# Attention with scratch-turned probabilities: a latent-attention and MoE layer on one NeuronCore

## What is computed

```python
q = heads(xn @ wq.T)                  # 16 heads of 64
latent = xn @ w_kv_down.T             # 64 wide, shared by all heads
k, v = heads(latent @ w_k_up.T), heads(latent @ w_v_up.T)
q, k = rotary(q), rotary(k)
scores = q @ k.T / 8 + causal_mask
probs = softmax(scores)               # float32
attention = concat(probs @ v) @ wo.T
# experts: sigmoid routing, top 4 of 16 (2 of 4 groups), up, silu, down,
# plus a shared expert of 256
```

## Time and profile before

| | us |
|---|---|
| span of the profiled execution (first to last instruction) | 640.2 |
| median of three runs | 641.15 |
| PE busy | 615.5 (96%) |
| DVE busy | 434.6 (68%) |
| ACT busy | 429.5 (67%) |
| POOL busy | 361.1 (56%) |

### The profile page before, as it was taken

The page is one execution under the profiler, slowest core; times in us unless marked ns, Lnnn a source line. Parts: engine busy times, 40 slices in busy tenths (PEclk is TensorE's granted clock), DMA queues, the critical chain, the costliest instruction groups (busy, mean ns, idle before and its releaser), DMA issues.

```text
span 640.2 us, 17380 instructions
## 1 busy us (share of the span) xinstructions
PE 615.5 (96%) x5302; PEld 511.2 (80%) x5302; DVE 434.6 (68%) x1250; ACT 429.5 (67%) x1036; POOL 361.1 (56%) x456
## 2 busy tenths in 40 slices
PE   2899999899999999999999999999999999999996
PEld 2666767688888888888888888888888888888884
DVE  5495556487758775877577757775777677766661
ACT  3364323377776777677767776877687768776763
POOL 2013111168846884688468846884688468843431
PEclk9599999999999999999999999999999999999999
DMA  9500004942484248324832483248424832483001
GB/s 256 147 21 2 1 1 106 205 108 47 106 207 97 46 105 210 90 49 103 210 89 49 104 211 86 50 106 210 118 53 103 211 84 54 102 212 84 2 2 34
DMA packets 35208, 65.29 MB, mean 102 GB/s; under 512 B 11104, under 2 KB 19312, under 8 KB 35056
## 3 DMA queue, kind: packets, MB, share of 16 engines
q1 hardware_dynamic: 32624, 63.53, 41.4%
q10 hardware_dynamic: 2560, 1.45, 0.9%
HBM read 5.84 MB, written 1.05 MB: 11 GB/s over the span
## 4 chain that ended last, share of the span: by engine, by line
PE 93%; DVE 3%; ACT 2%; DMA 1%; issue 1%; SPq 0%; DVEq 0%
PE ps L536 23%; PE ps L520 22%; PE ps L502 11%; PE ps L503 11%; PE ps L547 7%; PE ps L483 4%; PE ps L409 4%; PE ps L469 4%; PE ps L411 1%; PE ps L412 1%; PE ps L382 1%; PE ps L471 1%; DMA acc<-x 1%; PE ps L425 1%; PE ps L444 1%
## 5 line engine op out<-in xcount | busy, mean ns | idle before, releaser
L607 ACT ACTIVATE probsT<-ps 128x512 f32<-128x512 f32 (+3 forms) x256 | 131.8, 515 | 48.6 <-PE ps L520 44.8
L1023 POOL TENSOR_SCALAR probs_long<-probs_long,rden 128x1024 f32<-128x1024 f32 (+3 forms) x128 | 123.6, 966 | 66.1 <-DVE rden L923 65.5
L502 PE MATMUL ps<-ks,qs 128*128 128x512 f32 (+2 forms) x384 | 154.7, 403 | 3.0 <-DVE negmax L917 3.0
L536 PE MATMUL ps<-probsT,lat_now 128*64 128x128 f32 x2304 | 154.0, 278 | 0.0
L917 DVE CUSTOM_DVE_ANT_0 probs_long<-ps,mask 128x1024 f32<-128x1024 f32 (+3 forms) x128 | 130.8, 1022 | 27.7 <-PE ps L503 25.5
L536 PEld LDWEIGHTS ps<-probsT,lat_now 128*64 128x64 f32 x2304 | 123.2, 136 | 24.3 <-issue 18.9
L503 PE MATMUL ps<-ks,qx 128*128 128x512 f32 (+2 forms) x384 | 130.3, 347 | 0.0
L698 ACT ACTIVATE probs_long<-probs_long,negmax 128x1024 f32<-128x1024 f32 (+3 forms) x128 | 125.7, 982 | 2.2 <-DVE negmax L917 2.0
L1023 POOL TENSOR_SCALAR probs_short<-probs_short,rden 128x128 f32<-128x128 f32 (+3 forms) x128 | 68.6, 536 | 91.1 <-DVE rden L923 91.0
L520 PE MATMUL ps<-ident,probs_long 128*128 128x128 f32 x832 | 113.6, 273 | 0.3 <-ACT probsT L607 0.2
L520 PEld LDWEIGHTS ps<-ident,probs_long 128*128 128x128 f32 x832 | 96.8, 140 | 8.1 <-ACT probsT L607 2.5
(11 more groups left out here) (127 smaller groups left out, 750.5 us busy)
## 6 DMA issues: line engine op xcount, KB each, us to landing
qs<-roped SPq DMA_DIRECT2D x128, 128.0 KB, 2.4
qx<-roped SPq DMA_DIRECT2D x128, 128.0 KB, 2.4
ks<-roped SPq DMA_DIRECT2D x128, 128.0 KB, 2.5
lat_now<-lat SPq DMA_DIRECT2D x16, 256.0 KB, 2.5
wk_now<-wkT SPq DMA_DIRECT2D x9, 256.0 KB, 2.3
wq_now<-wqT SPq DMA_DIRECT2D x9, 128.0 KB, 2.0
acc<-x SPq DMA_DIRECT2D x2, 512.0 KB, 5.6
rope<-c_rope SPq DMA_DIRECT2D x1, 1024.0 KB, 11.9
```

Of the source, the lines that this page charges most:

```text
L502: nc.tensor.matmul(out_ps[:, lo:hi], qs[n][:, rows], ks[n][:, lo:hi], start=True, stop=False)
L536: last = nc.tensor.matmul(obank[HD * a:HD * a + HD, :], lat_now[p][:, kb, :], probsT[:, m % 2, a, kb * P:(kb + 1) * P], start=(kb == 0), s ...
L607: return nc.scalar.activation(dst, src, ACT.Copy, scale=scale)
L1023: nc.gpsimd.tensor_scalar(row, row, rden[:, m % 8:m % 8 + 1], 1.0, ALU.mult, ALU.mult)\
```

## The change

Experts and routing stay, apart from loops written out in place of hardware loops. Attention is rewritten around groups k = 0 to 63, with r = 0, 1 the two heads' long rows and r = 2, 3 the short ones:

- q and k stay f32 and are not split. The stack holds two heads in 128 rows, 64 rows each; `scores` makes one f32 matmul per head and 512 columns, over 64 rows, the two heads into different PSUM banks. SP's stacks become 8 DMAs of 256 KB for each unit.
- Long scores fill banks 0 to 3, short scores use banks 0 and 1 again. PE therefore starts a group's short scores after its long maxima, and the next long scores after its short maxima.
- The first five key blocks of each long row (10 of 18) are not turned by PE. DVE transposes 32x32 squares (`turn_fast`, 128x640 for each head), SP writes the result to an HBM scratch (640 KB) and, when that has landed, reads it back with four DMAs of 160 KB that put the squares in place (`exchange`). The other 8 blocks are transposed by PE and copied by ACT alone.
- The rows are not divided. ACT scales the projected result by the reciprocal (`scale_rows`, four 128x128 pieces), and POOL adds it to `acc`. For that the projection is made separately for each head, over 64 rows.

```diff
+            def exchange(k):
+                s = k % 2
+                sp.wait_ge(zig_done, 2 * k + 2)
+                if k >= 2:
+                    sp.wait_ge(in_fast[s], READS * (k // 2))
+                sp.dma_start(scratch[s], zig[s][:]...).then_inc(in_zig[s], 16)
+                sp.wait_ge(in_zig[s], 16 * (k // 2 + 1))
+                if k >= 2:
+                    sp.wait_ge(pv_done, k - 1)
+                by_query = scratch[s].rearrange("(q k) c n -> k q c n", q=4)
+                for ki in range(4):
+                    sp.dma_start(fastT[s][32 * ki:32 * ki + 32]...,
+                                 by_query[:, :, ki, :]).then_inc(in_fast[s], 16)
...
+            def scores(k, r, chunk):
+                p, width = pair_of(k), blocks_of(k, r) * P
+                rows = slice(width - P, width)
+                lo, hi = chunk * TB, min(chunk * TB + TB, width)
+                for a in range(2):
+                    half = slice(HD * a, HD * a + HD)
+                    to = long_ps(a)[:, lo:hi] if r == 0 else ps[:, a, lo:hi]
+                    mm = nc.tensor.matmul(to, qk[p][half, 0, rows], qk[p][half, 1, lo:hi], start=True, stop=True)
...
+            for k in range(-1, GRPS + 2):                 # TensorE
+                if k + 1 < GRPS:
+                    long_scores(k + 1)                    # waits max_done 4(k+1)
+                if k >= 2:
+                    project(k - 2)
+                if 0 <= k < GRPS:
+                    turn_slow(k)                          # waits exp_done 4k+4
+                if k + 1 < GRPS:
+                    short_scores(k + 1)                   # waits max_done 4(k+1)+2
+                if 1 <= k <= GRPS:
+                    products(k - 1)                       # waits slow_act, in_fast
+                for e in pieces_at(k):
+                    rotary(e)
...
+            for k in range(-1, GRPS + 2):                 # ScalarE
+                if k >= 2:
+                    copy_output(k - 2)
+                    scale_rows(k - 2)
+                if k + 1 < GRPS:
+                    softmax_exp(k + 1, 0)
+                    softmax_exp(k + 1, 1)
+                if 0 <= k < GRPS:
+                    copy_slow(k, 0)
+                    copy_slow(k, 1)
+                if k + 1 < GRPS:
+                    softmax_exp(k + 1, 2)
+                    softmax_exp(k + 1, 3)
...
+            for k in range(-1, GRPS + 2):                 # VectorE
+                if k >= 0:
+                    for e in pieces_at(k - 1):
+                        turn(e)
+                if k + 1 < GRPS:
+                    row_max(k + 1, 0)
+                    row_max(k + 1, 1)
+                if 0 <= k < GRPS:
+                    reciprocals(k)
+                if k + 1 < GRPS:
+                    row_max(k + 1, 2)
+                    row_max(k + 1, 3)
+                    turn_fast(k + 1, 0)
+                    turn_fast(k + 1, 1)
```

More of the change, by code:

```diff
@@ L45, with unit_of, pair_of, blocks_of @@
 LONG, SHORT = [7, 6, 5, 4], [0, 1, 2, 3]
[L46 to L74, removed]
-QW = S // 4
[L80 to L113, removed]
+RING = 4
+PAIRS = 2
+GRPS = 4 * PAIRS * UNITS
+FAST = 5
+SLOW = 4
+def unit_of(k):
+    return k // 8
+def pair_of(k):
+    return k % 8 // 4
+def blocks_of(k, r):
+    return (LONG if r < 2 else SHORT)[k % 4] + 1
+def ring_col(k, r):
+    return k % RING * 4 + r
+QW = S // 4
+PIECES = 8
+EARLY = 4
+def pieces_at(k):
+    if k == -1:
+        return [8, 9, 10]
+    if 0 <= k and k + 11 < PIECES * UNITS:
+        return [k + 11]
+    return []
+def quarter(e):
+    return slice(e % 4 * QW, e % 4 * QW + QW)
+def rope_bank(e):
+    return 6 + e % 2 if e < PIECES else 7
 PAD = E // 2
@@ L276, in stack @@
[L276 to L306, removed]
@@ L598, in _ @@
-            with pe.Fori(0, UNITS - 1) as u:
-                unit(u)
-            unit(UNITS - 1, last=True)
-            project(PROJECTIONS - 1, 2 * QUADS - 1, ALL_USES - 1, 16 * UNITS + 1, xbanks[(ALL_USES - 1) % 2])
+                    for a in range(2):
+                        half = slice(HD * a, HD * a + HD)
+                        last = nc.tensor.matmul(ps[:, 7 - a, c * P:(c + 1) * P],
+                                                oT[k % 2][half, c * P:(c + 1) * P], mix[half, m0, :],
+                                                start=True, stop=True)
+                        if c == 1:
+                            last.then_inc(proj_pe, 1)
@@ L892, in _ @@
             dve.wait_ge(in_rope, 16)
[L893 removed]
+            for w in range(PASSES):
                 for k in range(PASS_CH):
[L895 to L898 removed]
                     dve.wait_ge(silu_act, w * PASS_CH + k + 1)
@@ new lines, in add_head @@
+            def add_head(k, a):
+                lower_i, gap = SHORT[k % 4], LONG[k % 4] - SHORT[k % 4]
+                rows = acc[:, bass.ds(unit_of(k) // QUADS * QB + lower_i, 2, step=gap), :]
+                if 2 * k + a:
+                    pool.wait_ge(ad_done, 2 * k + a)
+                pool.wait_ge(scaled_done, 4 * k + 2 * a + 2)
+                nc.gpsimd.tensor_tensor(rows, rows, scaled[k % 2][:, a], ALU.add).then_inc(ad_done, 1)
+            for e in range(PIECES):
+                rotate(e)
```

548 lines of the change are left out of this document (197 added, 351 removed).

## The result

The changed kernel takes **654.35 us** (median of four runs, 649.80 to 657.84) against 642.39 us for the kernel before beside it (638.45 to 645.78): 1.017 times as long, 95% interval 1.011 to 1.024. That is slower, and clear of no change; whether the loss reaches 2% the interval leaves open. I had forecast 642, with 606 to 700 as the range. The profiled execution took 649.80 us, the shortest of the four.

A forecast was written before the change was run, and what follows sets the result against it. TensorE was taken as the bound: 6.93 us of work plus 0.97 of wait make 7.90 a group. 62 x 7.90 = 489.8, filling 12, draining 14, 122.1 ahead and 3.7 behind gave 641.6, forecast 642 us, range 606 to 700.

The forecast's parts named there:

- TensorE's work: TensorE's products, scores, transposes, projection and rotary piece in one attention group, without waits: 6.93 us.
- The drain rule: Changing tiling mode drains TensorE at stage borders: group 8.16 us, total 16 us higher; left out of the sum.
- The new wait: TensorE waits ahead of the short scores for both long maxima on VectorE: 0.97 us in every group.
- my first rival: The wait before the short scores shrinks: 582 us without any, 612 with half; chance 0.17.
- VectorE's transpose: VectorE's 128x640 f32 transpose, two per group: taken as 0.825 us each, upper bound 1.65.
- The third rival: VectorE's transposes take two passes: 8.5 to 8.7 us a group, 685 us total; chance 0.10.
- the fourth rival: Half-row tiles on TensorE do not overlap: scores + 2.1 us, projection + 0.4, total 778 us; chance 0.05.
- SP and the scratch: SP's write, reads and stacks take 7.2 us a group; scratch data, usable after some 8.5 of about 13, are covered.
- Two of my own signs: Signs for the forecast: no TensorE wait for the fast blocks, and SP waiting less than 4 us for each write.
- my second rival: The scratch exchange in SP's stream becomes the bound: group 9.5 us, total 742 us, halfway 692; chance 0.15.
- Filling: Start of attention: two iterations without products, three rotary pieces in one of them, 12 us.
- rivals 2 to 5: Scratch bound (0.15), two-pass transposes (0.10), half-row tiles not overlapping (0.05), removed transposes were hidden, 708 us (0.03).

The follow-up runs named there:

- e9: Changed kernel with stacks spread as 4 x 128 KB in four groups behind scratch writes, and the rotary piece before the short scores: 594.70 us.
- e5: Changed kernel with each of VectorE's two 128x640 transposes made twice, same result: 676.94 us, 1.056 times the kernel before.
- e6: Changed kernel with both heads' score products on the same half of the rows, which changes what is computed: 715.50 us.
- e8: Changed kernel with the stacks split into 4 x 128 KB in each of four groups of a unit, issued between scratch write and its landing: 621.17 us.
- e1: Changed kernel with SP issuing the next unit's stacks between a scratch write and the wait for its landing: 633.20 us.
- e11: Changed kernel with the stacks of units 1 to 7 issued by GpSimd instead of SP, at the same points: 636.23 us.

## Why the prediction was right, and where it was not

The total came out inside the range, 12 us above my number; to a slower kernel I had given a chance of 0.46. Cut as I had cut it, the profiled execution reads:

| | predicted | measured |
|---|---|---|
| ahead of attention | 122.1 | 116.8 |
| two filling iterations (116.79 to 137.37) | 12 | 20.6 |
| 62 full iterations (to 626.3) | 489.8 | 488.9 |
| draining, to the issue of the last store (644.37) | 14 | 18.1 |
| behind | 3.7 | 3.6 |
| sum | 641.6 | 648.0 |

The middle agrees to a microsecond, and that is partly luck: 7.90 us a group was forecast as even. It is 7.50 with 34 us of stalls in between, and the last ten full groups have no rotary piece, which I had charged to all: undisturbed they take 6.2 to 6.8 us, 10 us less together. 62 x 7.50 + 34 - 10 is 489.

- **TensorE's work**: 6.93 forecast, 6.79 measured in the window of four groups (30.02 less 2.87 of waits, over four). Products 2.11 (I had 2.25), scores 2.32 (2.6), transposes 0.88 (0.88), projection 0.61 (0.46), rotary 0.87 (0.74). The errors nearly cancel. The scores were dear in my sum because I charged a second head's rest behind both; the next stage starts into it. Against the scores of before at 2.6, they save 0.28. The projection is half-row tiles too and is slower than whole ones.
- **The drain rule** I had set against the change would have made a group 0.26 us longer. Here the short scores of four blocks hand over to 64-column products in 1.06 us from start to start (320.16 to 321.22 in e9), which is 4 x 0.2375 and the second head's 0.11. No run shows a price for the border beyond what my prices held.
- **The new wait**: 0.97 forecast for every group, 0.63 measured on the mean (1.20, 0.85, 0.37, 0.09), with 0.09 more ahead of the projection. It falls with the maximum's length, from 1.23 us at 8 blocks to 0.82 at 5, while the transposes behind which it hides stay at 0.88. The mean is lower than mine because both of its sides were mis-sized. The two maxima take 1.98 us on the mean of the four groups of the window, from the first start to the last end (2.38, 2.12, 1.84, 1.58), where I had 2.21: the second starts together with the first one's accumulator read. And from the start of the first, PE has 1.46 us of work until it could begin the short scores, where I had 1.24. This is a part of my first rival.
- **VectorE's transpose**: 0.825 forecast, 0.822 measured; the turn 1.22 and 1.223. The third rival is gone. e5 shows besides that two passes would have cost 23 us beside the stalls, less than my 43: VectorE had more in hand than I gave it.
- **Half-row tiles**: they overlap; e6 prices the fourth rival at 61 us for the scores alone, or 86 in a loop without stalls, where I had 136 with the projection. I let next to nothing of the longer scores vanish into waits, and 0.7 us a group did.
- **SP and the scratch: the step that failed.** I wrote "a unit's 8 stack DMAs 0.61 / group" and had SP at 7.2 us, "under 7.90 by 0.7", and the scratch data at 8.5 us of about 13, "Covered". The mean was about right: the write lands in 4.4 us (I had 3.9), four reads issue in 1.73 (2.45). But the eight stacks come as two bursts of 1 MB. In such a group SP issues stacks for 3.2 to 4.7 us, not 0.6, and the write behind them takes 5.1 to 8.0 us to land. The 4.5 us in hand would have covered eight small delays; they did not cover one large one. Two of my own signs showed it: PE was to have no wait for the fast blocks, and SP less than 4 us for each write, and the median is 4.4. It was my second rival in place and mechanism, at an eighth of its frequency: 34 us and not 100.
- **The clock** was in no term. A stall of 4.14 us costs 6.6 (13.74 against 7.12): behind it TensorE runs at 1.2 GHz for the products and the rotary piece (granted clock 0.50), 2.4 us more. The mean granted clock fell from 0.988 to 0.966.
- **Filling** cost 8.6 us more than I gave it. PE's first iteration:

```profile
121.24 0.49 PE L413 MATMUL ps<-qk 64*128 64x128 f32 x4 [2.46 <-DVE negmax L777]
121.66 1.13 PE L329 MATMUL ps<-xT,wqT 128*128 128x256 f32 x4
124.92 2.08 PE L329 MATMUL ps<-xT,wqT 128*128 128x256 f32 x4 [2.13 <-DVE prod L657]
128.38 2.07 PE L329 MATMUL ps<-xT,wqT 128*128 128x256 f32 x4 [1.39 <-DVE prod L657]
130.39 3.09 PE L413 MATMUL ps<-qk 64*128 64x512 f32 x8
```

Three rotary pieces share one PSUM bank. Each waits until VectorE has turned the one before, 3.3 to 3.5 us for one instead of 0.74. The second and third run at 1.2 GHz after those waits (granted clock 0.50), in 2.1 us where the first took 1.13.

- **The chances** have a slip: with 0.03 moved each way out of rivals 2 to 5 they are 0.31, 0.25 and 0.44, not 0.30, 0.24 and 0.46.
- **Ahead of attention** the same work took from 116.4 to 122.5 us in the thirteen traces, in two clusters with nothing between 117.1 and 121.4, in changed kernels of the same code up to there. The profiled execution of the changed kernel, at 116.8, was in the short one, and that of the kernel before, at 122.1, in the long one. Five microseconds of the comparison of the two traces are this and no part of the change. What decides between the clusters no run shows.

The ledger against the kernel before: 64 groups 0.49 us shorter, -31.4; stalls at the stacks, +34; the ends of attention beyond 64 even groups, 527.6 - 64 x 7.50 - 34 = 13.6 in place of 3, +10.6; the start, -5.3. Sum +7.9, and the spans differ by 7.8. The third term is what is left over, so the sum closes by itself; it holds the filling and draining, less the ten groups without a rotary piece. e8 takes out the second term and is 33 us faster than the changed kernel; e9 shortens the group further and is 60 us faster.

## What to carry to other kernels

A queue's load must be added up for its worst period, not for the mean: work that comes in bursts is paid by the one iteration in which it falls, and if that iteration's data has a deadline, the whole loop stops for it. When a wait is to be filled, use work whose own inputs are there already, and ask what the work moved in front makes late: 1.1 us of products in the same hole cost 24 us, a rotary piece of 0.9 us gained 26. The two differ in what they wait for and a little in length, and no run tells these apart. And a loop that gets faster shortens the time that every hidden transfer has, so the second repair shows its worth only after the first. Last, ask of each listed wait whether the engine named had not long been done: here the page put the waits for the scratch to "issue" and to ScalarE, and e1's long groups, which look like the changed kernel's, were another wait.

## What the runs showed of the hardware

- A 32x32-square transpose of f32 on VectorE, 128x640, takes 822 ns, as long as the maximum over 640 (825 ns in the earlier trace rows).
- Two f32 products over 64 rows, one on each half, take 1.82 us for 16 blocks of 128x128; on the same half 3.54, with 0.42 of other work in it (e6).
- A DMA's issue on SP takes 0.42 us for a read of 160 KB (1.73 for four) and 0.65 for a stack of 256 KB (medians). Four stacks took 3.2 to 4.9 us, and four reads right behind them up to 4.08 (e1). From GpSimd four such stacks were issued in 2.13 us (e11). What slows the issue on SP no run shows.
- The 640 KB write lands in 2.9 us from issue at its best, in 4.4 on the median, and behind or beside a 1 MB burst in 5.1 to 8.0 in the changed kernel and in up to 8.7 in e11.
